# A graph network kernel whose two relational hops are worked in blocks of 64 edge tiles instead of 32, on one Trainium2 core

## The reference

```python
hyper_head = expmap0(head_emb)
hyper_tail = expmap(tail_emb, hyper_head)
hyper_rel = expmap(rel_emb, hyper_head)
res = project(mobius_add(hyper_tail, hyper_rel))
res = logmap(res, hyper_head) + ricci * 1e-07      # ricci = normalised (tail_emb + rel_emb)
res = jax.nn.relu(res)
sums = zeros.at[head].add(res); counts = zeros.at[head].add(1.0)
return sums / clip(counts, 1.0)
# between hops: x = normalised result of the hop, ent = 0.5 * ent + x
```

## Time and profile before

| | |
|---|---|
| median of 3 runs | 24083.2 us |
| profiled execution: its own time / its span | 24039.33 / 24037.5 us |
| DVE busy in the span | 16546.3 us (69%) |
| PE busy (weight loads beside it) | 10326.4 us (43%), 6860.3 us (29%) |
| POOL busy | 12605.7 us (52%) |
| ACT busy | 2139.0 us (9%) |
| hop 1, hop 2 | about 16471 to 20169 us and 20276 to 23978 us of the span |

### The profile page before, as it was taken

The page is one execution under the profiler, slowest core; times in us unless marked ns, Lnnn a source line. Parts: engine busy times, 40 slices in busy tenths (PEclk is TensorE's granted clock), DMA queues, the critical chain, the costliest instruction groups (busy, mean ns, idle before and its releaser), DMA issues. The chain is left out here.

```text
span 24037.5 us, 205919 instructions
## 1 busy us (share of the span) xinstructions
PE 10326.4 (43%) x47565; PEld 6860.3 (29%) x47566; DVE 16546.3 (69%) x26071; ACT 2139.0 (9%) x3670; POOL 12605.7 (52%) x12782
## 2 busy tenths in 40 slices
PE   0033326655555555556666422222333333333333
PEld 0033322222222222222222322222333332333332
DVE  8744439988888888886666211115888886878887
ACT  0011110000000000000000000001111111111111
POOL 0188876655566555536665166653444443444443
PEclk9999997555555555558887555555555555555555
DMA  4133331111111111121112001113111112111112
GB/s 170 25 69 69 69 64 25 24 23 23 22 21 23 23 23 23 22 20 24 24 24 23 9 21 21 21 21 49 52 51 50 51 50 41 52 51 50 52 50 42
DMA packets 1118452, 942.42 MB, mean 39 GB/s; under 512 B 775931, under 2 KB 887579, under 8 KB 1117875
## 3 DMA queue, kind: packets, MB, share of 16 engines
q0 software_dynamic: 419904, 437.84, 9.9%
q1 hardware_dynamic: 698096, 500.67, 8.0%
HBM read 726.46 MB, written 207.32 MB: 39 GB/s over the span
## 5 line engine op out<-in xcount | busy, mean ns | idle before, releaser
L1420 POOL DMA_INDIRECT tail<-ball,h_idx x3328 | 3271.7, 983 | 1793.3 <-issue 1231.1
L736 PE MATMUL p_rad<-w_stack,hid_t 99*128 99x512 bf16 (+1 forms) x6656 | 3079.6, 620 | 2391.3 <-DVEq L826 1161.0
L808 DVE TENSOR_REDUCE red<-prod 128x96 f32<-128x1536 f32 x1664 | 2898.3, 1742 | 3.5
L1098 POOL DMA_INDIRECT l_xg<-h_tab,l_idx x1664 | 1571.2, 944 | 1444.1 <-issue 828.3
L1452 PE MATMUL h_sum<-head,h_hot 128*128 128x64 f32 x6656 | 1444.2, 421 | 1987.4 <-ACT head L1498 1987.4
L1438 PE MATMUL h_head<-ball_parts,hot_t 128*128 x9984 | 1067.6, 281 | 2813.4 <-issue 1578.1
L337 POOL DMA_INDIRECT rec_a<-rec,slot x1600 | 1990.4, 1244 | 517.2 <-issue 500.5
L692 POOL DMA_INDIRECT rec_b<-l_rcb x1600 | 1920.0, 1200 | 571.6 <-issue 570.5
L930 POOL DMA_INDIRECT l_xg<-x_tab,l_idx x1664 | 1571.6, 944 | 1141.8 <-issue 874.0
L946 PE MATMUL l_sum<-outer,l_hot 128*128 128x512 f32 x3328 | 1693.3, 673 | 945.6 <-DVEq L991 869.7
L736 PEld LDWEIGHTS p_rad<-w_stack,hid_t 99*128 99x128 bf16 (+1 forms) x6656 | 774.5, 132 | 4337.7 <-issue 4336.0
(11 more groups left out here) (369 smaller groups left out, 18896.7 us busy)
## 6 DMA issues: line engine op xcount, KB each, us to landing
hot_t<-rows_l SPq DMA_DIRECT2D x208, 512.0 KB
rec_a<-fill SPq DMA_DIRECT2D x128, 728.0 KB, 19.6
l_rec<-rec_a SPq DMA_DIRECT2D x104, 896.0 KB, 4.8
rhot_t<-rows_r SPq DMA_DIRECT2D x208, 384.0 KB
tail<-ball,h_idx POOLq DMA_INDIRECT x3328
t<-in_type SPq DMA_DIRECT2D x100, 500.0 KB
l_xg<-in_x,l_idx POOLq DMA_INDIRECT x1664
l_xg<-x_tab,l_idx POOLq DMA_INDIRECT x1664
```

What stands on the lines that cost most here:

```text
L736: ins = pe.matmul(p_rad[j % 2][:, h * 512:(h + 1) * 512], hid_t[j // 4 % 2][0:K3 + 3 * (1 - i), j % 4, i, :], w_stack[i][0:K3 + 3 * (1 - i ...
L808: ch.step(dve.tensor_reduce(red[:, j, :], prod[j % 3][:, :, :], AX, ALU.add))
L1420: pool.indirect_dma_start(tg[q][:, j, :], None, table[:, :], bass.IndirectOffsetOnAxis(ap=idx[q][:, j:j + 1], axis=0)).then_inc(gathered[q ...
```

## The change

- **Blocks of 64 tiles.** `HU = 4` units of 16 tiles make a block; there are 26 blocks. `idx` and a new buffer `ends` (head lanes and relation numbers) are loaded by SP per block from two tables in DRAM (`list_i`, `list_e`), which `rows_phase` writes; POOL's copy is gone. POOL starts a unit's 16 gathers when the unit's tails have been used; it waits after every eighth gather as before.
- **The chain in halves.** `op` now issues each instruction twice, for the first and the second 32 tiles; an instruction waits for the last but one, which is its own half's predecessor.
- **Single buffers.** `head` and `rel` in SBUF are single, the relation buffer in PSUM too (`p_rel`; `rel_taken` tells PE when it is free). So the picks of block b+1 stand behind the sums of block b, and ScalarE's copies behind its Relus.
- **Map words.** PE reads the eight words of block b+1 two by two ahead of each unit's sums of block b.
- **Relation term.** `rel * c` leaves DVE; ScalarE does it tile by tile, 64 instructions of 64 columns with a scale per partition (`relations`).
- **hots** are built per 8 tiles in two alternating buffers during the results. `compares` of the next block's units 0 and 1 and its relation one-hots take their former places in the chain's gaps; units 2 and 3 are compared after the adds.
- **Elsewhere.** Node features are not kept in SBUF through the hops: they are stored to `x_kept` by the normalisation and loaded again; `ent` is loaded and stored around the unite stage. Two earlier stages share their semaphores, cleared after use.

```diff
+HU = 4
 def hop_phase(...):
-        W, Q, H = 2 * BT, BT // 2, BT // 4
+        W, Q, H, N2 = HU * BT, HU * BT // 4, BT // 4, HU * BT // 2
-        hg = [sb(f"head{q}" + tag, [P, W, T_PICK]) for q in range(2)]
-        rg = [sb(f"rel{q}" + tag, [P, W, D + 2]) for q in range(2)]
+        hg = sb("head" + tag, [P, W, T_PICK])
+        rg = sb("rel" + tag, [P, W, D + 2])
-        p_rel = [ps(f"h_rel{k}" + tag, [P, 4, P]) for k in range(2)]
+        p_rel = ps("h_rel" + tag, [P, 4, P])
...
         @block.gpsimd
-                    hold(pool, turn, tails_used, b + 1)
-                    ch.do(pool.tensor_copy(idx[q][:, :], g["dst_b"][:, bass.ds(b * W, W)]))
+                    hold(pool, turn, idx_in[q], it * 16 + 16)
                     for j in range(W):
+                        if j % BT == 0:
+                            hold(pool, turn, tails_used, b * HU + (j // BT + 1))
...
         @block.tensor
             def body(b, q, it, left):
-                if left:
-                    pick(b + 1)
                 hold(pe, turn, added, b + 1)
                 for j in range(W):
                     if j % BT == 0:
+                        if left:
+                            chunk.extend(words(b + 1, j // BT))
                         hold(pe, turn, relu_done, ...)
...
+                if left:
+                    pick(b + 1, chunk)
...
         @block.scalar
+            def relations(u):
+                for j in range(u * BT, u * BT + BT):
+                    ins = act.activation(rg[:, j, 0:D], rg[:, j, 0:D], ACT.Copy, scale=sc[:, 19, j:j + 1])
+                ins.then_inc(scaled, 1)
...
+                relations(0)
+                for u in range(HU):
+                    if u < HU - 1:
+                        relations(u + 1)
+                    hold(act, turn, asked, b * (5 + HU) + (6 + u))
+                    act.activation(hg[:, z, 0:D], hg[:, z, 0:D], ACT.Relu).then_inc(relu_done, 1)
                 if left:
+                    quads(b + 1)
...
         @block.vector
                 def op(f):
-                    ch.sync()
-                    ch.step(f(S, S2, E, B2, z))
+                    for half in range(2):
+                        z = slice(half * (W // 2), (half + 1) * (W // 2))
+                        if ch.n > 1:
+                            dve.wait_ge(chain_s, ch.n - 1)
+                        ch.step(f(S, S2, E, B2, z))
...
+                for u in range(HU):
+                    z = unit(u)
+                    for vec, c in ((h, 16), (t, 18)):
                         ch.step(tt(vec[:, z, 0:D], vec[:, z, 0:D], bc(sc[:, c, z].unsqueeze(2), big), MUL_))
+                    load_chunks()
                     ch.sync()
+                    ch.step(tt(h[:, z, 0:D], h[:, z, 0:D], t[:, z, 0:D], ADD))
+                    load_chunks()
+                    ch.sync()
+                    dve.sem_inc(tails_used, 1)
+                    dve.wait_ge(scaled, b * HU + (u + 1))
                     ch.do(tt(h[:, z, 0:D], h[:, z, 0:D], r[:, z, 0:D], ADD))
                     dve.sem_inc(asked, 1)
+                    for m in range(2):
+                        hots(q, b, 2 * u + m)
+                for u in range(HU):
+                    dve.wait_ge(sum_done, b * (2 * HU) + (2 * u + 2))
+                    add_groups(dve, ch, chunk[u * BG:u * BG + BG], acc, ...)
+                dve.sem_inc(added, 1)
                 if left:
+                    compares(b + 1, 2)
+                    tails(1 - q, it + q)
+                    compares(b + 1, 3)
+                    heads(1 - q, b + 1)
```

More of the change, by code:

```diff
@@ L1358, in _ @@
         def _(sp):
-            store_nodes(sp, x_kept, g["x"], D, stored)
+            w = NT // list_i.shape[1]
+            sp.dma_start(list_i, g["dst_b"][:, :].rearrange("p (b w) -> p b w", w=w)).then_inc(stored, 16)
+            for k, name in enumerate(("lane_b", "rel_b")):
+                sp.dma_start(list_e[:, :, k, :], g[name][:, :].rearrange("p (b w) -> p b w", w=w)).then_inc(stored, 16)
             sp.wait_ge(split, 1)
@@ L1423, in _, with words @@
                             hold(pool, turn, gathered[q], it * (16 * W) + 16 * (j + 1))
-                    ch.restart()
         @block.tensor
         def _(pe):
[L1428 to L1442, removed]
+            def words(b, u):
+                return [c for i in range(2) for c in chunks(pe, g["map"][1], b * (N2 // PACK) + 2 * u + i)]
@@ L1500, in _ @@
             act.activation(p_row[:, 0:P], g["row"][:, :], ACT.Copy).then_inc(row_ready, 1)
             act.sem_inc(taken, SEED)
-            for k in range(Q):
-                quad(0, 0, k)
+            act.sem_inc(rel_taken, 1)
+            quads(0)
             all_blocks(act, NW, body)
@@ L1546, in heads, with unit, compares @@
-            def heads(q, b, meanwhile=lambda: None):
-                dve.wait_ge(taken, b * Q + (Q + SEED))
-                h, t, r = hg[q], tg[q], rg[q]
+            def unit(u):
+                return slice(u * BT, u * BT + BT)
+            def compares(b, u):
+                h = u % 2
+                dve.wait_ge(rows_in[h], (b * 2 + (u // 2 + 1)) * 32)
+                ch.step(ts(hot_t[h][:, :, :], hot_t[h][:, :, :], g["lane"][:, 0:1], None, ALU.is_equal))
+                ch.step(ts(rhot_t[h][:, :, :], rhot_t[h][:, :, :], lane_rel[:, 0:1], None, ALU.is_equal))
+                ch.sync()
+                dve.sem_inc(hot_done, 1)
@@ L1591, in body @@
                 dve.sem_inc(asked, 1)
-                hots(q, b, 0)
+                if left:
+                    compares(b + 1, 0)
+                    compares(b + 1, 1)
                 dve.wait_ge(told, b * 4 + 1)
@@ L1643, in body @@
                 dve.sem_inc(asked, 1)
-                hots(q, b, 1)
+                if left:
+                    relation_hots(1 - q, it + q)
                 dve.wait_ge(told, b * 4 + 2)
@@ L1699, in body, with load_chunks @@
                 ch.sync()
+                dve.sem_inc(asked, 1)
                 big = [P, BT, D]
-                for half in range(2):
-                    z = slice(half * BT, half * BT + BT)
-                    for vec, c in ((h, 16), (t, 18), (r, 19)):
+                chunk = []
+                def load_chunks():
+                    chunk.extend(chunks(dve, g["map"][1], b * (N2 // PACK) + len(chunk) // PACK))
+                for u in range(HU):
+                    z = unit(u)
+                    for vec, c in ((h, 16), (t, 18)):
```

329 lines of the change are left out of this document (176 added, 153 removed).

## The result

The changed kernel takes 23841.4 us (median of 4 runs, 23814.8 to 23885.2), the kernel before 24087.6 (4 runs): ratio 0.9898, 95% interval 0.9881 to 0.9916. That is 246 us faster where 493 were forecast; in the two profiled executions it is 208 (23831.7 against 24039.3). The direction and nearly all terms were right. One term was not, the time of a quad of picks, and it took half of the forecast gain.

A forecast was written before the change was run, and what follows sets the result against it. DVE was taken to set the period of 140.0 us per 64 tiles; 33.8 + 1.6 + 42 + 5.2 + 16q, q = 2.9, gives 129.0. With hop edges and +33 outside, 23,590 us; range 22,960 to 24,280.

The forecast's parts named there:

- 42 + 0.6: After the chain: last sum 42 us after it, then 0.6 until the first quad of picks.
- 4.0 + 0.6 + 1.6: Block's end: 4.0 us of heads for the last unit, 0.6 for the last copy, 1.6 for the loop's jump.
- q: Time of one of a block's 16 quads of picks: 2.9 us, bounded by 2.0 and 3.6.
- the 0.3 for the words: Picks: map words leave the path, taking 0.3 us off block 0's 3.2 a quad.
- a part of the picks may see none: Picks in the hops: gathers end after 96 us of the block, argued against the slower hand-over rival.
- The +0.42 for the single buffer: Picks: 0.42 us a quad that two relation buffers overlapped, added to 2.9 for the upper end, 3.6.
- longer than 1.5 us each: POOL's gathers: growth beyond 1.5 us each was named as a sign of the prediction being wrong.
- The fast rival: Picks flow at PE's own pace, q = 2.0: period 116.4 us, 22,960 us; chance 0.15.
- The slow rival: Hand-over between PE, ScalarE and DVE slower than in block 0: q = 3.8, 24,310 us; chance 0.15.
- break-even of 3.5: Picks: the q at which the change gains nothing, with a period of 138.9 us.
- The chain rival: DVE's chain is not halved, taking 41.8 us: period 144.6, 24,370 us; chance 0.07.
- the bound of 0.256 from a Tanh row: ScalarE's scaling: 32 instructions at no more than 0.256 us each, 8.2 us ahead of the first Relu.

The follow-up runs named there:

- e1: The changed kernel with seven of eight gathers of tail rows left out in the hops, those rows staying constant: 22605.6 us in one run.
- e6: The changed kernel with two PSUM relation buffers, DVE reading the lane numbers from SBUF: 23795 us, ratio 0.9883.
- e12: Changed kernel, POOL waiting before a block's 33rd gather for the previous block's picks, trains of 16 after, tails before third unit's compares: 22977 us, ratio 0.9655.
- e7: The changed kernel with each chain instruction issued once for all 64 tiles instead of in halves: 23945 us, ratio 0.9952.
- e2: The changed kernel with POOL waiting after every sixteenth gather instead of every eighth: 25120 us, ratio 1.044.

## Why the prediction was half right

*By its own terms, for hop 1.* Measured and forecast: chain 34.5 against 33.8; results to the first copy 44.4 against 42 + 0.6 and the first copy's own delay; last copy to the next chain 6.9 against 4.0 + 0.6 + 1.6. Everything but 16q is right within 1 us (136.5 - 16 x 3.38 = 82.4 against 82.6). The first chain of a hop came 128.1 us after its start instead of 70.0: +58.1, forecast +60. Last block to unite 79.1 instead of 56.6: +22.5, forecast +22.7. Outside the hops the profiled executions differ by 22 before the fourth layer, 16, 9 and 4 around node tables, unite and the end, together +51 against +33; some of the 22 may be no effect at all, since runs of one kernel spread by more than that.

*The step that failed* is the size of q: the prediction read the time of a quad in block 0, where nothing else runs on PE and ACT, and used it for every block. It named the picks as what eats the gain and bounded q by 2.0 and 3.6, but then took 2.9, and 2.5 to 3.3 as its own range. In the blocks it is 3.38, so the 50 intervals cost (3370.8 - 3225.0) + (3353.1 - 3225.0) = 274 us more, nearly the whole miss of 285 in the profiled executions.

For block 0 itself 2.9 was right. The first and the last copy of relation rows of the changed kernel's block 0, with the map words off the path and one relation buffer:

```profile
16525.43 0.39 ACT L1505 ACTIVATE rel<-h_rel 128x264 f32<-128x264 f32 x1 [15.68 <-PE h_rel L1474]
...
16567.57 0.39 ACT L1505 ACTIVATE rel<-h_rel 128x264 f32<-128x264 f32 x1 [0.91 <-PE h_rel L1474]
```

That is (16567.57 - 16525.43) / 15 = 2.81, and 2.84 in hop 2. So the 0.3 for the words is not what failed, but the step from block 0 to the others. Two things differ there, and the trace prices one. In e1, almost without gathers, a quad takes 1.44 in block 0 and 1.60 later: the later blocks wait in the middle of their picks for the rows of the third and of the fourth unit (3.9 and 3.7 us between two copies instead of 1.2), block 0 for one of them; that is 2.4 of the 8 us. The rest comes with the trains: the prediction argued that "a part of the picks may see none", since gathers fill only 96 us of a block. But POOL's start hangs on `tails_used`, and its idle time lies beside the chain; 32 of a block's 64 gathers, four trains, are issued during its 16 quads, 26 in block 0. Why the trains cost a later block more than that, no run separates. The +0.42 for the single buffer, in the upper end, was wrong (e6: 0.1).

The gathers were also longer than 1.5 us each, which the prediction had named as a sign of being wrong: (2300 - 587.2) / 1080 = 1.59. It did not set the period, since POOL still idles 35 us a block:

```profile
L1451 POOL DMA_INDIRECT tail<-ball,h_idx x1080 | 1109.2, 1027 | 1192.1 <-DVEq L1761 587.2 <-issue 455.0 <-DMA tail<-ball,h_idx 149.9
```

*The fast rival* (q = 2.0, 22,960) is what e1 shows: 1.6 a quad, interval 112.0 where 116.4 was worked out. Its condition was not met in the changed kernel because of the gathers, and is nearly met in e12. *The slow rival* named the right mechanism, a hand-over slower than in block 0, and the right break-even of 3.5; the case came within 0.12 of it. Its reason, the single relation buffer, was not the cause (e1, e6). *The chain rival* is out: e7, and pairs start 0.27 apart. The Trainium skill (VectorE: DVE Perf Modes, "The TRN2 errata — SBUF-src ops pay a fixed extra latency per instruction") says that every small tile pays the latency. Two independent halves do not show that here: an instruction of 32 columns lasts 0.19 us, and the other half's starts 0.12 after it. One piece of twice the width took 37.7 us where the halves take 34.5 (e7).

ScalarE's scaled copies start 0.24 us apart in the changed kernel's timeline (6.55 / 27), below the bound of 0.256 from a Tanh row:

```profile
17633.62 6.55 ACT L1510 ACTIVATE rel<-rel,sc 128x64 f32<-128x64 f32 x27 [1.30 <-DVEq L1745]
```

The estimate from the Trainium skill's figures (ScalarE: Activation LUTs, "What ACT_TABLE_LOAD costs") was 0.24 as well, and the trace agrees.

*What the profile of before could have told.* The lateness was in it: the earlier trace rows shows two copies released from "remote" in stretches where POOL issues gathers. I wrote that I could not name it. Laid beside POOL's timeline, the first of the two starts after a train's last gather, the second within a train. And over both hops of the kernel before, 559 of 826 signals of `picked` came more than 1 us after the end of their matmul, by up to 6.9 us; with two buffers and a whole block of time, nobody waited for them.

## What to carry to other kernels

Before a change moves a hand-over between two engines onto the path that sets the end, look at how late the receiving engine starts today, not only at how long the work takes, and at what else runs in that moment. A wait that is hidden now has no price in the profile, only a lateness. If the lateness lines up with trains of indirect gathers, move the gathers to a stretch where nobody waits for TensorE, with a wait of POOL for the phase to pass. Where somebody waits for TensorE, shorter trains (4 here) helped as long as POOL had time to spare. Beside DVE's chain one train of 16 behind a train of 8 was cheap (0.7 us), 16 behind 16 cost 7 us, and 24 cost 13. And a time read in a hop's first block is the first block's: before it is multiplied by the number of blocks, ask what stands beside the same work in the others.

## What the runs showed of the hardware

- Signals of completed matmuls reached ScalarE and DVE late while trains of eight indirect gathers of 128 rows ran: 367 of 693 by more than 1 us, at most 8.4, and none of the 121 outside. With four gathers in a train the most was 4.4 us, with 16 it was 24.6. With one gather in eight 831 of 832 came within 0.1 us, and a quad took 1.60 us instead of 3.38. With trains of 16 the results stage lost 35 us a block.
- In the same stretches the signals that ScalarE and DVE raise were on time (over 1 us late: 6 of 1788 and 2 of 12390; 6 and 2 in e1 as well), and nearly so beside e2's trains of 16 (6 of 1935 and 8 of 13164). The chain took 34.2 us with hardly any gathers and 35.5 with 21 to 23 of them beside it in trains of 8.
- From the 18th gather of a train of 24 on, DVE's signal to itself was late too (pairs 0.7 us apart instead of 0.22), and beside the chain from the 12th or 13th of a train of 16 that follows a train of 16. Why, no run here shows. That the train before counts would fit a queue that fills, which was not tested.
- Two independent DVE instructions of 64 columns on the same tile start 0.14 us apart and of 32 columns 0.12 (medians over both hops), each lasting 0.18 to 0.22.
